# Attention rows updated out of PSUM, a mask moved between two subtractions, unit transposes in the score ring, and edge tiles converted by two engines

## What is computed

```python
def _L0_gnn_ref(x, adj, beta):
    norm2 = jnp.linalg.norm(x, axis=1, keepdims=True)
    cos = beta[0] * (x @ x.T) / (norm2 @ norm2.T + 1e-07)
    masked = cos + (1.0 - adj) * -1000000000.0
    P = jax.nn.softmax(masked, axis=1)
    return P @ x

def _L1_gnn_ref(h, adj, W_self, W_neigh):
    deg = jnp.clip(jnp.sum(adj, axis=1, keepdims=True), 1.0)
    h_neigh = adj @ h / deg
    return h @ W_self + h_neigh @ W_neigh
h = jnp.maximum(_layernorm(x, axis=-1), 0.0)
x = x + _L0_gnn_ref(h, adj, L0_gnn_beta)
h = jnp.maximum(_layernorm(x, axis=-1), 0.0)
x = x + _L1_gnn_ref(h, adj, L1_gnn_W_self, L1_gnn_W_neigh)
return x
```

## Time and profile before

| | us |
|---|---|
| median of three runs (517.0 to 521.71) | 518.51 |
| the profiled execution | 520.0 |
| its span, first to last instruction | 518.2 |
| of this, TensorE busy | 478.1 |
| ScalarE busy | 325.1 |
| VectorE busy | 301.4 |
| GpSimd busy | 265.4 |

### The profile page before, as it was taken

The page is one execution under the profiler, slowest core; times in us unless marked ns, Lnnn a source line. Parts: engine busy times, 40 slices in busy tenths (PEclk is TensorE's granted clock), DMA queues, the critical chain, the costliest instruction groups (busy, mean ns, idle before and its releaser), DMA issues.

```text
span 518.2 us, 12726 instructions
## 1 busy us (share of the span) xinstructions
PE 478.1 (92%) x5392; PEld 402.6 (78%) x5392; DVE 301.4 (58%) x701; ACT 325.1 (63%) x459; POOL 265.4 (51%) x222
## 2 busy tenths in 40 slices
PE   1777899999999999999989999999889999999996
PEld 1654788888778887788778877877678988888895
DVE  6973555657855569566865695787772313231253
ACT  2969797886998769987798699688541111101111
POOL 3848676775767557765686577676552000000000
PEclk9888899999999999999999999999899999999999
DMA  8055676554777546764675467552010000000001
GB/s 244 0 205 196 197 239 210 198 201 174 231 249 225 184 152 225 276 205 136 226 269 193 147 215 243 199 189 84 22 33 1 23 22 17 5 22 22 22 2 40
DMA packets 31547, 74.37 MB, mean 144 GB/s; under 512 B 2560, under 2 KB 15104, under 8 KB 31488
## 3 DMA queue, kind: packets, MB, share of 16 engines
q1 hardware_dynamic: 31488, 73.54, 42.8%
HBM read 71.43 MB, written 2.10 MB: 142 GB/s over the span
## 4 chain that ended last, share of the span: by engine, by line
PE 74%; ACT 13%; DVE 8%; issue 2%; POOL 1%; DMA 1%; ACTq 0%; SPq 0%; DVEq 0%
PE ps L1040 22%; PE ps L899 12%; PE ps L910 8%; ACT word L527 6%; PE ps L937 5%; PE ps L940 5%; PE ps L963 5%; PE ps L960 5%; PE ps L939 5%; PE ps L962 5%; ACT ps L528 5%; DVE far L758 3%; PE ps L1026 2%; PE ps L1015 2%; DVE adj_t L606 1%
## 5 line engine op out<-in xcount | busy, mean ns | idle before, releaser
L388 POOL TENSOR_TENSOR near<-word,adj_t 128x1024 f32<-128x1024 f32 x72 | 144.8, 2012 | 105.6 <-PE ps L963 79.0
L527 ACT ACTIVATE word<-ps,small 128x512 f16<-128x512 f32 x144 | 135.4, 940 | 58.8 <-PE ps L899 58.3
L748 DVE TENSOR_TENSOR word<-ps,word 128x512 f16<-128x512 f32 x144 | 107.0, 744 | 112.0 <-ACT ps L528 111.8
L1040 PE MATMUL ps<-table,adj_t 128*128 128x257 f16 x1024 | 116.8, 274 | 0.0
L899 PE MATMUL ps<-unit_t 128*128 128x512 f16 x432 | 107.5, 381 | 9.1 <-DVE word L748 7.6
L1040 PEld LDWEIGHTS ps<-table,adj_t 128*128 128x128 fp8e4 x1024 | 99.4, 98 | 12.9
L528 ACT ACTIVATE ps<-ps,small 128x512 f32<-128x512 f32 x144 | 107.0, 743 | 0.0
L960 PE MATMUL ps<-table,near 128*128 128x129 f16 x576 | 103.3, 220 | 2.6 <-POOL near L388 2.6
L963 PE MATMUL ps<-table,near 128*128 128x129 f16 x576 | 103.5, 223 | 0.0
L962 PE MATMUL ps<-table,near 128*128 128x128 f16 x576 | 103.3, 220 | 0.0
L937 PE MATMUL ps<-table,far 128*128 128x129 f16 x448 | 81.8, 223 | 9.1 <-DVE far L758 9.1
(11 more groups left out here) (93 smaller groups left out, 514.3 us busy)
## 6 DMA issues: line engine op xcount, KB each, us to landing
stage<-in_adj_dram SPq DMA_DIRECT2D x128, 512.0 KB, 4.3
x_sb<-in_x_dram SPq DMA_DIRECT2D x4, 512.0 KB, 6.2
x_again<-in_x_dram SPq DMA_DIRECT2D x8, 256.0 KB, 5.1
out_dram<-x_sb SPq DMA_DIRECT2D x7, 256.0 KB, 2.3
out_dram<-x_sb SPq DMA_DIRECT2D x1, 192.0 KB, 2.0
stage<-in_L_gnn_W_neigh_dram SPq DMA_DIRECT2D x1, 64.0 KB, 2.5
stage<-in_L_gnn_W_self_dram SPq DMA_DIRECT2D x1, 64.0 KB, 2.6
out_dram<-x_sb SPq DMA_DIRECT2D x1, 64.0 KB, 1.5
```

What stands on the lines that cost most here:

```text
L388: pool.tensor_tensor(ring(near, k), ring(word, k), adj_t[:, near_adj(k)], ALU.mult).then_inc(s_near, 1)
L527: act.activation(half(word16, k, c, 0, HIGH, TPS), score(k, c), ACT.Exp, bias=exp_bias, scale=exp_scale)
L748: dve.tensor_tensor(half(word16, k, c, 0, LOW, TPS), score(k, c), half(word16, k, c, 0, HIGH, TPS), ALU.subtract).then_inc(s_elo, 1)
L1040: return pe.matmul(ps[:, agg_bank(g) + t, 0:TW], adj_t[:, at:at + P], tab(b), start=(b == 0), stop=(b == T - 1))
```

## The change

Five parts.

1. **Ring.** The transposes of strips 3 to 7 move from the start into the main loop, each after the scores of the pair two ahead (k = 2, 4, ... 10). A list `RING` orders score chunks and transposed strips as items; each takes bank 5 + its place modulo 3 and waits for the item three places earlier. ScalarE's copy and VectorE's remainder move with them. Scores of a pair of strip 0 wait only for the strip that they read.
2. **Order at the start.** GpSimd writes the unit rows of strip 0 directly behind their norms and those of strip 7 as well; ScalarE writes strip 3 alone; VectorE strips 1, 2, 4, 5, 6. The flag is made from the least norm instead of the largest inverse norm. The sum of h goes to bank 1 and is cut into three parts between the transposes.
3. **New rows out of PSUM.** `evacuate` and `new_rows` become one block at the first pair of the next strip: the sums are formed in PSUM in place, the denominator and the four row updates read PSUM, and `s_evac` is signalled behind the updates. Statistics and aggregates each come a pair earlier. The copy of the means goes, and the variances plus epsilon are made by GpSimd.
4. **Mask between the subtractions.** `mask_far(k+1)` goes ahead of `low_part(k+2, 1)`.
5. **Two engines convert the far tiles.** GpSimd takes those of even number (with the near tile, three pairs ahead), ScalarE those of odd number.

```diff
+    RING = [("unit", 0), ("unit", 1), ("score", 0, 0), ("score", 0, 1), ("score", 1, 0), ("score", 1, 1), ("unit", 2)]
+    for k in range(2, NP):
+        RING += [("score", k, 0), ("score", k, 1)]
+        if k % 2 == 0 and 3 <= k // 2 + 1 < NS:
+            RING += [("unit", k // 2 + 1)]
+    AT = {item: i for i, item in enumerate(RING)}
...
-            return (5, 6, 7, 4, 3, 2, 0, 1)[g]
+            return 5 + AT["unit", g] % 3
...
-            def evacuate(s):
+            def new_rows(s):
                 dve.wait_ge(s_pvd, FIRST[s + 1])
+                if s >= 1:
+                    dve.wait_ge(s_spill, FAR_BEFORE[FIRST[s]])
                 for b in range(2):
                     rows = x_v3[:, s * TPS + 2 * b:s * TPS + 2 * b + 2, 0:D + 1]
-                    if s == 0:
-                        dve.tensor_tensor(rows, two_rows(acc_bank(s, b)), no_edge_two, ALU.add).then_inc(s_evac, 1)
-                    else:
-                        dve.wait_ge(s_spill, FAR_BEFORE[FIRST[s]])
-                        dve.tensor_tensor(rows, two_rows(acc_bank(s, b)), rows, ALU.add).then_inc(s_evac, 1)
-            def new_rows(s):
-                dve.wait_ge(s_evac, 2 * (s + 1))
-                then(dve.tensor_scalar(den_s, x_v3[:, s * TPS:(s + 1) * TPS, D], HS, None, ALU.mult))
+                    total = two_rows(acc_bank(s, b))
+                    last = dve.tensor_tensor(total, total, no_edge_two if s == 0 else rows, ALU.add)
+                then(last)
+                then(dve.tensor_scalar(den_s.rearrange("p (b h) -> p b h", h=2), denominators(s), HS, None, ALU.mult))
                 then(dve.reciprocal(rden, den_s))
                 dve.wait_ge(s_xr, 16 * (s + 1))
                 for t in range(TPS):
-                    row = x_row(s * TPS + t)
-                    last = dve.scalar_tensor_tensor(row, row, rden[:, t:t + 1], x_again[:, t * D:(t + 1) * D], ALU.mult, ALU.add)
-                last.then_inc(s_x2, 1)
+                    ins = dve.scalar_tensor_tensor(x_row(s * TPS + t), acc(s, t, 0, D), rden[:, t:t + 1],
+                                                   x_again[:, t * D:(t + 1) * D], ALU.mult, ALU.add)
+                    if t % 2 == 1:
+                        ins.then_inc(s_evac, 1)
...
                         low_part(k + 2, 0)
                     if PAIR[k][2]:
                         spill(k)
+                    if k + 1 < NP and PAIR[k + 1][2]:
+                        mask_far(k + 1)
                     if k + 2 < NP:
                         low_part(k + 2, 1)
-                    if k + 1 < NP and PAIR[k + 1][2]:
-                        mask_far(k + 1)
+                    if k % 2 == 0 and 3 <= k // 2 + 2 < NS:
+                        unit_low(k // 2 + 2)
...
                 if k + LEAD < NP:
                     convert(k + LEAD)
+                    if PAIR[k + LEAD][2] and FAR_BEFORE[k + LEAD] % 2 == 0:
+                        convert_far(k + LEAD)
...
-                    if k + 2 < NP and PAIR[k + 2][2]:
+                    if k == 1:
+                        unit_high(2)
+                    if k % 2 == 0 and 3 <= k // 2 + 1 < NS:
+                        unit_high(k // 2 + 1)
+                    if k == 0 or k % 2 == 1 and (k + 1) // 2 < NS:
+                        table_high((k + 1) // 2)
+                    if k + 2 < NP and PAIR[k + 2][2] and FAR_BEFORE[k + 2] % 2 == 1:
                         convert(k + 2)
...
+            def ring_free(*item):
+                at = AT[item]
+                if at >= 3:
+                    last = RING[at - 3]
+                    if last[0] == "unit":
+                        pe.wait_ge(s_ulo, last[1] + 1)
+                    else:
+                        pe.wait_ge(s_elo, 2 * last[1] + last[2] + 1)
...
-            sum_of_h(0, T - TX)
+            sum_of_h(0, TX)
             unit_transpose(0)
+            sum_of_h(TX, T - TX)
             unit_transpose(1)
+            scores(0)
             sum_of_h(T - TX, T)
+            scores(1)
             unit_transpose(2)
...
                 if k + 2 < NP:
                     scores(k + 2)
+                    if k % 2 == 0 and 3 <= k // 2 + 2 < NS:
+                        unit_transpose(k // 2 + 2)
```

More of the change, by code:

```diff
@@ L207, in score @@
         def score(k, c):
-            return ps[:, 5 + (2 * k + c) % 3, :]
+            return ps[:, 5 + AT["score", k, c] % 3, :]
         def turned(k, c):
@@ L388, in mask_near, with units, convert_far @@
                 pool.tensor_tensor(ring(near, k), ring(word, k), adj_t[:, near_adj(k)], ALU.mult).then_inc(s_near, 1)
+            def units(g):
+                pool.wait_ge(s_rnorm, g * TPS // TX + 1)
+                for t in range(g * TPS, (g + 1) * TPS):
+                    pool.tensor_scalar(u_rows(t, t + 1), h_rows(t, t + 1), rnorm[:, t:t + 1], HS, ALU.mult, ALU.mult
+                                       ).then_inc(s_unit_p, 1)
+            def convert_far(k):
+                m = FAR_BEFORE[k]
+                pool.wait_ge(s_far_in[0], (m // 2 + 1) * 16)
+                if m == FAR_BEFORE[FIRST[2]]:
+                    pool.wait_ge(s_tab, NS)
+                    pool.wait_ge(s_mean, 1)
+                pool.tensor_scalar(far_adj(k, adj_tb), stage[:, 2 * TILE:3 * TILE].rearrange("p (t c) -> p t c", t=TPS),
+                                   FP8_ONE, 0.0, ALU.mult, ALU.add).then_inc(s_adjt_p, 1)
             inverse_std(0)
@@ L631, in norms, with units @@
                 dve.tensor_scalar(norm2_g[:, part], norm2[:, part], 1e-20, None, ALU.max).then_inc(s_norm2, 1)
[L633 to L636 removed]
+            def units(g):
+                dve.wait_ge(s_rnorm, g * TPS // TX + 1)
+                for t in range(g * TPS, (g + 1) * TPS):
                     dve.tensor_scalar(u_rows(t, t + 1), h_rows(t, t + 1), rnorm[:, t:t + 1], HS,
@@ L893, in score_product @@
                 s, p, _ = PAIR[k]
-                q = 2 * k + c
-                if i == 0 and q >= 3:
-                    pe.wait_ge(s_elo, q - 2)
+                if i == 0:
+                    ring_free("score", k, c)
+                    if s == 0 and p * 2 % TPS == 0:
+                        pe.wait_ge(s_ulo, p * 2 // TPS + 1)
                 j = unit_lo(2 * p + c, 1) if i == 0 else unit_hi(2 * p + c, 1)
```

194 lines of the change are left out of this document (90 added, 104 removed).

## The result

The changed kernel took 503.68 us (median of 4 runs, 502.79 to 504.55), the kernel before beside it 517.75 (4 runs, 516.99 to 521.71). The ratio is 0.971, with a 95% interval of 0.966 to 0.977: faster by about 3%. The profiled execution took 502.87 us, with a span of 500.9. The forecast was 501, its range 496 to 509.

A forecast was written before the change was run, and what follows sets the result against it. TensorE, busy 92% of 518.2 us, was taken as the bound, so only its waits could go: start 4.4, boundaries 7.2 and end 6.0 sum to 17.6 us, taking the median from 518.5 to 500.9, say 501; range 496 to 509.

The forecast's parts named there:

- the three places: Where TensorE stands still and time can be gained: the start, four strip boundaries and the end of attention; 17.6 us together.
- both rivals of a smaller gain: Start gives nothing (15%, 505.3 us) and boundaries and end give half (14%, 507.5 us); together the range's high end, 509.
- The start: Before the even pace: unit transposes in the ring and reordered unit rows gain 4.4 us, between 0 and 7.
- Its first subtraction starts at 34.9: At the start, VectorE's first subtraction waits behind 4 + 12 unit rows, with three GpSimd meetings of 0.5 to 0.6 us.
- the start gives nothing: Rival, 15%: VectorE's 12 unit rows each meet a GpSimd instruction, costing 4.8 us and the start's gain; 505.3 us.
- The ring: Rival, 5%: in strip 0 the ring holds TensorE 1 to 2 us for each of five transposed strips; 508 us.
- The boundaries: At four strip boundaries, 2 us lost each shrinks to 0.2: gain 1.8 x 4 = 7.2 us.
- what is left of the wait is 0.1 each: At a strip boundary, TensorE's two waits for mirrored masks, about 1.0 us each, shrink to 0.1 each.
- ScalarE is the late one at one place of a boundary: Two activations and a conversion stand ahead of an exponential; removing the conversion's 1.0 us is part of the 2 lost.
- The end: Strips 5 to 7: of 9.0 us lost, 3.0 stay for the last pair; gain 6.0 us, between 3 and 8.
- nothing of it is left: At the end, the 4.2 us lateness of the last pair's scores vanishes with a 2.4 us block at the strip's head.
- Slower: Rival, 4%: updates out of PSUM still exclude GpSimd's instructions; block 5.4 us, TensorE stands 15.3 us at six heads; 525.4 us.

The follow-up runs named there:

- e7: Changed kernel with the next pair's words turned ahead of a diagonal pair's near products, and GpSimd converting near tile 1 earlier: 500.44 us, .967 of the kernel before.
- e3: Changed kernel with all far conversions back on ScalarE: 503.99 us, .971 of the kernel before.
- e2: Changed kernel with new rows summed into SBUF and divided and updated at their old, later place: 513.02 us, .988 of the kernel before.
- e10: Kernel before with only the mirrored mask moved between the subtractions: 516.40 us, .995 of the kernel before.
- e1: Changed kernel with the mirrored mask put back behind the second subtraction: 512.04 us, .985 of the kernel before.
- e4: Changed kernel with the new-row block still at the strip's head, but its sums written to and read from SBUF: 514.68 us, .989 of the kernel before.
- e8: Changed kernel run again without any edit, on the chip of another set of runs: 503.77 us, .973 of the kernel before.

## Why the prediction was right, and where its steps were wrong

The time came within 3 us, inside the range, by three gains in the three places. That the spans differ by 17.3, where 17.6 was forecast, is luck: 3.0 of it is the clock, and by the medians the change gave 14.1. One term was a little too small and two were too large, the end most of all. The range held, though its high end was added up wrongly: "both rivals of a smaller gain" make 500.9 + 4.4 + 6.6 = 511.9, not 509.

**The start: 4.4 forecast, 6.4 measured, 4.8 without the clock, and the cause half missed.** The prediction gave the start to parts 1 and 2 alone. Above, the mask's place by itself gives 1.5 of it beside the clock, and the new start, once the others are in, 1.3 to 1.6 up to pair 16 and 1.0 in the median. "What binds the start" had to be asked for every part. Its single steps, in the timeline of the changed kernel:

```profile
18.95 1.11 PE L929 MATMUL ps<-ident,adj_t 128*128 128x128 f32 x4 [3.68 <-POOL adj_t L413]
19.86 5.18 PE L1013 MATMUL ps<-adj_t 128*128 128x128 f32 x32
25.31 1.46 PE L941 MATMUL ps<-unit_t 128*128 128x512 f16 x6
28.80 0.92 ACT L561 ACTIVATE word<-ps,small 128x512 f16<-128x512 f32 x1 [1.52 <-POOL small L441]
28.88 2.54 DVE L675 TENSOR_SCALAR adj_t<-adj_t 128x128 f32<-128x128 f32 x12 [0.24 <-issue]
29.70 1.87 POOL L413 TENSOR_SCALAR adj_t<-adj_t 128x128 f32<-128x128 f32 x4
31.54 1.33 DVE L778 TENSOR_TENSOR word<-ps,word 128x512 f16<-128x512 f32 x2
31.66 2.06 POOL L398 TENSOR_SCALAR adj_t<-stage 128x1024 uint8<-128x1024 f32 x2
37.66 1.06 ACT L538 ACTIVATE adj_t<-stage 128x1024 uint8<-128x1024 f32 x1 [1.46 <-DMA stage<-in_adj_dram]
```

- Strip 0 turned at 19.0: right. The sum of h between, "near the slow one" of 3.6 and 7.2: it was 5.18, in two paces (last section). Scores of pair 0 at 25.3 instead of 27.5, exponentials at 28.8 instead of 30.
- "Its first subtraction starts at 34.9": it was 31.54. The three meetings with conversions did not happen. The 12 unit rows (28.88 to 31.42) ran beside GpSimd's inverse norm and unit rows and cost 0.21 each, and the three GpSimd conversions that were counted beside them began only at 31.66. The order of GpSimd's list, which puts them last, was there to be read. With it fell the cause that the rival "the start gives nothing" named: unit rows beside unit rows hardly stall.
- Of those 3.4 us only 1.7 arrived at pair 5 (50.33 in the chain for the predicted 52). A wait that was not in the count stands between: ScalarE stood 1.46 us for far tile 3, whose transfer was issued at 33.10, behind the end of GpSimd's near conversion 1 at 32.7, and took 4.54 in the chain. e7 converts that tile earlier and has ScalarE's conversion at 36.77 without a wait, yet reaches pair 5 only 0.3 earlier, with its first exponential 0.36 later; so the wait seems to explain less than half of what was lost, and the rest was not taken apart.
- The ring: from pair 5 to 16 are 54.2 us with the old start and 56.47 with the new one, 2.3 for four turned strips where 1.9 was "only moved". Holding costs 0.1 a strip, not the 1 to 2 of the rival.

**The boundaries: 7.2 forecast, 6.2 measured.** The block was right to a tenth: 2.3 us for 2.4, a sum back to PSUM at 0.43 for 0.41, updates at 345 ns for 344. The term "what is left of the wait is 0.1 each" was too small: it is 0.2 at each of two masks (pairs 21 and 23 take 4.25 and 5.13, in e7 4.06 and 4.93). The mask (1.23, and the waits on both sides) must fit under the next scores (1.29), and the words are turned right before these. The wait is on the weight load, so it stands in that row (the load's idle time, of which TensorE feels the 0.2):

```profile
PEld ps L979 <- DVE far L788: 5.7, 11, 0.5
```

e7 gives the mask 1.37 more cover, and the loss is gone. "ScalarE is the late one at one place of a boundary ... part of the 2" was wrong outright: e3 has the conversions back on ScalarE and loses the same 0.46, and e2 with shared conversions loses what e10 does without. And the step that gave each part a share of the boundary could not be right: e1, e2 and e10 each leave the boundary at 2.0. Nor were they two waits for masks of "about 1.0 each": before, 0.30 of it was a wait for a subtraction (the table under e2).

**The end: 6.0 forecast, 4.8 measured, 3.4 without the clock.** This is the term that was furthest off. Of the 9.0 us that it called lost, 1.4 was no wait: TensorE was busy at half clock from 368.5 to 371.3, ahead of the scores at 372.62 that the prediction calls "4.2 late". The strip-5 boundary kept 0.4. And of "nothing of it is left" of the lateness, 0.85 was left. VectorE at the head of strip 6:

```profile
343.59 0.77 DVE L735 TENSOR_TENSOR ps<-ps,x_sb 128x258 f32<-128x258 f32 x2
...
344.80 1.13 DVE L741 SCALAR_TENSOR_TENSOR x_sb<-ps,small,x_again 128x128 f32<-128x128 f32 x4
345.84 0.74 DVE L778 TENSOR_TENSOR word<-ps,word 128x512 f16<-128x512 f32 x1
```

The exponentials were ready at 345.2 (ScalarE's L562 from 344.45, 0.72), the subtraction came at 345.84 behind the block. In a strip of four pairs, two of them diagonal, there seems to be less slack for those 2.3 us than in strip 1. The wait of the last pair stayed, as forecast (2.6 us behind GpSimd's near mask before and after, 3.0 taken).

**The other rivals.** GpSimd did not become the bound: it waits 56.4 us for VectorE. "Slower" was excluded by the right row (L773 of before, never over 0.432), and e4 shows its price: block 4.1 where it assumed 5.4, 8.2 us of TensorE's waiting where it assumed 15.3, and still 1% faster than before. Of the signs, "updates of a strip at 1.1, the 128x4 at 0.16" held exactly, strip 1 took 64.9 us for 64.6, the even pace came at 50.3 for 52, and attention ended at 363.4 for 363; "no wait of TensorE for mirrored words" did not hold.

## What to carry to other kernels

Where an engine's wait comes back with equal size when either of two edits is undone, the two waits covered each other: price the stretch with all but one removed, never share it out. Before counting busy TensorE time as lost or as work, read the granted clock there: a stretch at half clock in the one trace at hand is not a wait that an edit removes. A VectorE instruction that stalls beside GpSimd can be cured by the memory that it reads: from PSUM the same block at the same place took 2.3 us instead of 4.1. Under a cover of the same length as the work, a hand-over of 0.2 us stays open; look for an independent product that can go behind the producer.

## What the runs showed of the hardware that was not expected

- A VectorE instruction of 128x4 values cost 1.45 us beside a GpSimd mask when it read SBUF, and 0.16 beside the same mask when it read PSUM. It ended with GpSimd's mask (119.88 and 119.85), small as it is; the eight of them took 0.17 to 1.46.
- Unit rows on VectorE (128x128 out of SBUF) beside unit rows of GpSimd: 12 in 2.54 us, none of the kernel's 20 over 0.32, where the earlier trace rows has 8 in 2.22 with one conversion and the longest of that kernel took 0.86. The Trainium skill, page "SBUF — State Buffer", section "Who interferes with whom", has the shared ports taken for the whole instruction; the rows show that with short instructions on both sides little of it is felt.
- The same kernel has stretches at half clock in one execution and not in another. TensorE by windows (start:end us, busy (instructions), granted clock, DMA share, GB/s), the changed kernel first, then its repeat e8:

```profile
362.60:366.00 3.40, 3.40 (x40) 1.00 0.41 116
```

```profile
362.60:366.00 3.40, 3.40 (x28) 0.51 0.41 116
```

Both had just stood 2.6 us for the last pair's words. The kernel before and e10 also differ in clock at the two stretches of the section on the result, with longer waits ahead of them in the former (1.72 and 0.89 us against 0.28). This moves a time by 1 to 3 us, as much as some parts of this change.
- The sum of h in the changed kernel ran in two paces, and the granted clock doesn't show it:

```profile
19.00:22.90 3.90, 3.90 (x19) 1.00 0.00 0
22.90:25.00 2.10, 2.10 (x21) 1.00 0.25 41
```

0.2 us apiece in the first window, 0.1 in the second, at a clock given as full in both. The first is the pace of half clock in the earlier trace rows (16 in 3.62); whether that was the clock, no run shows; the pace of the instructions has to be read beside the granted clock.
